# A fused attention and expert block: the experts' weights loaded behind the stores of all batches, one more batch normalised by VectorE, the later tiles' deviations taken earlier

## What is computed

```
h = layernorm(x) * (1 + ca) + sa
x = x + ga * attention(h, Wq, Wk, Wv)      # 16 heads of 8, one key/value head
h = layernorm(x) * (1 + cb) + sb
x = x + gb * experts(h)                    # 8 experts, the best two per token, 128 -> 512 -> 128
```

## Time and profile before

| | |
|---|---|
| three timed runs, median (lowest, highest) | 623.52 us (622.25, 624.11) |
| the profiled execution | 620.85 us |
| its span | 619.0 us |
| mean granted clock of TensorE | 0.971 |
| busy: TensorE, VectorE, ScalarE, GpSimd | 90%, 80%, 72%, 52% |

### The profile page before, as it was taken

How to read it: one execution, slowest core, us unless ns; L and a number is a source line. 1 busy time by engine, 2 the same in 40 slices (tenths; PEclk the granted TensorE clock), 3 DMA queues, 4 the chain that set the end, 5 groups by cost and what they waited for, 6 DMA issues and landing times.

```text
span 619.0 us, 18924 instructions
## 1 busy us (share of the span) xinstructions
PE 557.3 (90%) x6699; PEld 307.3 (50%) x6699; DVE 495.7 (80%) x1132; ACT 444.6 (72%) x776; POOL 323.1 (52%) x576
## 2 busy tenths in 40 slices
PE   3677999999999999999999999999889999899970
PEld 2222333443443343343343344343369998799970
DVE  5767999989789789879788888878767777656687
ACT  5575488888778788978887877878766555467771
POOL 2525101034455666667667666765417767755670
PEclk9797999999999999999999999999899999999995
DMA  7973400120120220230130030000123223232645
GB/s 197 334 230 115 131 8 12 41 66 13 41 64 19 67 72 17 54 84 18 36 103 18 22 109 21 23 27 26 45 57 99 76 83 95 84 100 68 200 137 174
DMA packets 49868, 49.32 MB, mean 80 GB/s; under 512 B 15616, under 2 KB 44336, under 8 KB 49056
## 3 DMA queue, kind: packets, MB, share of 16 engines
q1 hardware_dynamic: 42256, 36.89, 21.5%
q0 software_dynamic: 4320, 9.38, 4.6%
q10 hardware_dynamic: 3200, 1.84, 1.0%
HBM read 29.40 MB, written 17.10 MB: 75 GB/s over the span
## 4 chain that ended last, share of the span: by engine, by line
PE 68%; DVE 16%; ACT 6%; issue 3%; POOL 2%; DMA 2%; SPq 0%; POOLq 0%; DVEq 0%; ACTq 0%
PE ps L1095 15%; PE ps L1054 13%; PE ps L1085 12%; DVE neg_max L1400 10%; PE ps L1163 10%; PE ps L1174 9%; ACT P L1262 3%; ACT diag L1272 2%; PE ps L1122 1%; PE ps L1137 1%; PE ps L1154 1%; PE ps L1073 1%; POOL h_sorted L809 1%; DVE P L286 1%; PE ps L469 1%
## 5 line engine op out<-in xcount | busy, mean ns | idle before, releaser
L1400 DVE TENSOR_REDUCE neg_max<-ps 128x1 f32<-128x512 f32 x512 | 321.1, 683 | 54.5 <-PE ps L1054 53.5
L1262 ACT ACTIVATE P<-ps,zero 128x1024 f32<-128x1024 f32 x256 | 272.3, 1112 | 72.5 <-PE ps L1085 72.2
L1054 PE MATMUL ps<-K,Q 128*32 128x512 bf16 x2048 | 183.3, 383 | 4.9 <-DVE neg_max L1400 4.5
L1085 PE MATMUL ps<-Q,K 128*32 128x512 bf16 x2048 | 155.9, 381 | 5.5 <-ACT P L1262 5.1
L1095 PE MATMUL ps<-P,V 128*32 128x512 f32 x1024 | 134.1, 598 | 1.2 <-ACT P L1262 1.1
L1054 PEld LDWEIGHTS ps<-K,Q 128*32 128x32 bf16 x2048 | 54.5, 96 | 108.7 <-DVE neg_max L1400 59.8
L1612 POOL DMA_INDIRECT y_rows<-P,to_now x71 | 73.8, 1040 | 61.0 <-DVE P L1452 28.6
L1318 ACT ACTIVATE parts<-ps,parts 128x128 f32<-128x128 f32 x228 | 65.1, 371 | 40.3 <-PE ps L1163 40.3
L1085 PEld LDWEIGHTS ps<-Q,K 128*32 128x32 bf16 x2048 | 52.4, 97 | 75.6 <-issue 28.8
L809 POOL DMA_INDIRECT h_sorted<-diag,slot x64 | 64.8, 1013 | 28.6 <-POOL max_parts L79 13.4
L1163 PE MATMUL ps<-parts 128*128 128x128 f32 x456 | 61.0, 277 | 2.6 <-DVE parts L1433 1.3
(11 more groups left out here) (239 smaller groups left out, 583.3 us busy)
## 6 DMA issues: line engine op xcount, KB each, us to landing
Q<-q_parts SPq DMA_DIRECT2D x24, 384.0 KB
xs<-h_sorted SPq DMA_DIRECT2D x71, 72.0 KB
W<-w_t SPq DMA_DIRECT2D x2, 2048.0 KB, 10.7
q_parts<-parts SPq DMA_DIRECT2D x8, 384.0 KB, 3.9
Q<-y_rows SPq DMA_DIRECT2D x6, 512.0 KB, 4.5
diag<-att_u SPq DMA_DIRECT2D x128, 16.0 KB
Q<-max_parts SPq DMA_DIRECT2D x96, 4.0 KB, 1.8
out<-Q SPq DMA_DIRECT2D x6, 256.0 KB, 2.3
```

What stands on the lines that cost most here:

```text
L1054: ins = eng.matmul(ring_bank(*unit)[QUAD * q:QUAD * (q + 1), :], Q[buffer_of(g)][:, g % NG * G + j, at:at + QUAD], K[buffer_of(g)][:, 0, : ...
L1085: ins = eng.matmul(bank(2 * u + j)[QUAD * q:QUAD * (q + 1), :], K[p][:, 1, at:at + QUAD], Q[p][:, g % NG * G + 2 * u + j, :], start=True, ...
L1262: nc.scalar.activation(P[s % 2][:, 2 * u:2 * u + 2, :], bank(2 * u, 2).rearrange("p (j t) -> p j t", j=2), ACT.Exp, bias=zero[:], scale=SC ...
L1400: eng.tensor_reduce(neg_max[g % 2][:, j * T + s:j * T + s + 1], ring_bank("maximum", g, s, j), AX.X, ALU.max, negate=True).then_inc(ring_u ...
```

## The change

It has three parts. The four loads of the experts' weights move on SyncE from ahead of batch 0's store to behind the store of batch 7, and the two waits ahead of them go. `VECTOR_FIRST` becomes 4: VectorE normalises all four tiles of batch 3, and does so inside `take(0)`, between its two kinds of subtractions, no longer at the head of `take(1)`. The root of the later tiles' variances moves on ScalarE from behind `mid(1)` to behind `modulate(2)`, and its reciprocal on VectorE from ahead of `take(2)` to ahead of `take(1)`. The order of everything else stays.

```diff
-        VECTOR_FIRST = 3
+        VECTOR_FIRST = 4
...
-            eng.wait_ge(loaded, START + LOADED)
-            eng.wait_ge(x_arrived[-1], START + 16)
-            eng.dma_start(W1[:, :, 0:F], w1_t).then_inc(experts_loaded, 16)
-            eng.dma_start(W1[:, :, F:F + FC], b1_t).then_inc(experts_loaded, 16)
-            eng.dma_start(W2[:], w2_t).then_inc(experts_loaded, 16)
-            eng.dma_start(W1[:, :, F + FC:], b2.partition_broadcast(128)).then_inc(experts_loaded, 16)
             store(eng, 0)
             eng.wait_ge(cleared, START + 4)
             eng.wait_ge(stored[0], START + STORES)
             load_operands(eng, 0, 0, batch_loaded)
             for b in range(1, B):
                 store(eng, b)
+            eng.dma_start(W1[:, :, 0:F], w1_t).then_inc(experts_loaded, 16)
+            eng.dma_start(W1[:, :, F:F + FC], b1_t).then_inc(experts_loaded, 16)
+            eng.dma_start(W2[:], w2_t).then_inc(experts_loaded, 16)
+            eng.dma_start(W1[:, :, F + FC:], b2.partition_broadcast(128)).then_inc(experts_loaded, 16)
...
                 mid(b)
-                if b == 1:
+                if b + 2 < B:
+                    modulate(b + 2)
+                if b == 0:
                     eng.wait_ge(var1_done, START + 16)
                     deviations(LATER)
-                if b + 2 < B:
-                    modulate(b + 2)
                 if b + 1 < B:
                     hi(b + 1)
...
-                if b + 2 < B:
+                if b != 1 and b + 2 < B:
                     eng.wait_ge(var_done, known(b + 2))
                     eng.wait_ge(xT_done, START + b + 1)
                     normalize(eng, b + 2, first_xn, by_vector(b + 2))
...
                     eng.tensor_tensor(rest_of(b, n), projected(b, n), part(b, n, 0), ALU.subtract).then_inc(rest_done, 1)
+                if b == 0:
+                    eng.wait_ge(xT_done, START + 2)
+                    normalize(eng, 3, first_xn, by_vector(3))
...
             for b in range(B):
-                if b == 2:
+                if b == 1:
                     eng.wait_ge(std_done, START + 3)
                     eng.reciprocal(ln_rstd[:, LATER], ln_rstd[:, LATER]).then_inc(var_done, 1)
                 take(b)
```

## The result

| | before | changed |
|---|---|---|
| median of 5 timed runs (lowest, highest) | 623.52 us (622.25, 624.11) | 618.48 us (618.13, 620.76) |
| ratio to before, 95% interval | | 0.9924 (0.9908 to 0.9940) |
| the profiled execution, its span | 620.85, 619.0 | 618.48, 616.6 |
| mean granted clock of the profiled execution | 0.971 | 0.977 |

The changed kernel is faster by 5.0 us, 0.8%. The forecast was 619.6 us (616.8 to 622.6), a gain of 3.9.

A forecast was written before the change was run, and what follows sets the result against it. The opening stage, with TensorE's idle stretches and half clock, was taken to set the chain's end. Front 3.9 us, stores, reload, weights and later stages 0: 617.0 us against the profiled execution, 619.6 against the median, range 616.8 to 622.6.

The forecast's parts named there:

- What bounds the kernel: Whole span: TensorE carries 68% of the last-ending chain, DMA 2%; any gain comes from the opening stage and reaches the end.
- Batch 3 on VectorE: Opening stage: VectorE's tiles end near 22.15 us, so batch 3's transposes start at 22.2, 1.7 us earlier.
- GpSimd's tiles: Opening stage: two normalisations took 1.06 us each from 21.71; batch 4's two start at 23.4 and take 1.6 to 2.1.
- Deviations ahead: Opening stage: later tiles' reciprocal at 23.1 us without waiting; batch 4's transposes near 26.45 against 29.93, 3.5 us earlier.
- The clock: TensorE's turn for batch 4: full speed adds 1.65 us to 3.5, 5.1 in all; 3.9 taken, bounds 1.8 and 5.1.
- fourth rival: Behind 46 us: half clock lasts longer or falls in a busier place, 3.3 us eat nearly all the gain; chance 0.08.
- Weights behind the stores: SyncE's queue: removing four issues frees nothing that was ready, and the weights' new place costs 0; bounds -0.5 and +5 us.
- The reload and batch 1's store: SyncE: reload issued from 27.5 to 29 us, ahead of the first maximum; batch 7's copies about even, at worst 1 us.
- second rival: First maximum waits for batch 0's reload, or batch 7's copies for batch 1's store; gain 1.9 us, 621.6; chance 0.08.
- shift(0) behind the weights: SyncE's queue: its transfers queue behind the weights' rest, land near 63 us, wanted at 68.4; the 5 us gap hides it.
- Against the median: Whole kernel: the profiled execution lies 2.7 us under the median 623.52, so 617.0 becomes a forecast of 619.6 us.

## Why the prediction was right, and where not

- **What bounds the kernel.** Right. The two idle stretches, their causes and the half clock between them were where the gain was, and the attention handed the front's lead on to the experts' stage to a tenth of a microsecond.
- **Batch 3 on VectorE.** Right to 0.1 us: transposes forecast at 22.2, seen at 22.15; the idle stretch 1.06 us against 1.2.
- **GpSimd's tiles.** The reading of 1.06 us each was an average over unlike ones: one took 1.33 us, the other 0.79. After the change batch 4's two took 0.81 and 0.83 us, the lower end of the 1.6 to 2.1 allowed. The slow one (21.71 to 23.04) began beside VectorE's wide subtraction for the last parts (L418, 21.66 to 22.35), and so did every slow one in both front traces (1.0 to 1.33 us); beside VectorE's normalisations and first subtractions they took 0.79 to 0.86. So sharing shows here beside one kind of VectorE instruction and not beside the others.
- **Deviations ahead.** Right: reciprocal forecast at 23.1, seen at 22.92; batch 4's transposes 26.45, seen 26.30.
- **The clock.** The sum's mis-sized term. I took 3.9 us, near the floor; the profile gives 5.1 by the first maximum, the upper bound, because the 2.0 us idle stretch did not lower the clock. Three other profiles with the same front lost it there, so the edge was rightly seen and the side wrongly chosen. That the clock is worth this much is shown: with only the clock held and the old order, the gain by the ratios is as large. The fourth rival, a longer half clock behind the front, did not come: it lasted about 7 us both before (from 46.8) and after (from 42.2).
- **Weights behind the stores, priced 0.** Right for the move alone (0.2%), wrong for its part in the change, and hidden by a sum that came out near. The step read who waited for SyncE's row before and found nobody; it did not ask who would wait once the front is 4 to 5 us faster and the weights are still early. The run with the weights early shows it: by the ratios 3.7 of 4.7 us go. The move makes room for the gain rather than giving one, and so does issuing batch 1's store first.
- **The reload and batch 1's store** (second rival). The store landed in 2.4 us instead of the 4.7 assumed, so the reload started 1.1 to 2.6 us before the forecast's 27.5 to 29. "About even; at worst 1 us" for the copies of batch 7 was right: 0.6 us.
- **shift(0) behind the weights.** Forecast to land near 63 without being waited for. Its last transfer landed by 62.9 and nobody waited. The three took 3.1 to 3.5 us to land instead of 1.8, and so landed about when the last of the weights did (62.2), which is nearer to the queue's order than to mere sharing. Loads of this size can hold up a shift all the same, as the run with the weights further back shows, at a price of 14 us.
- **Against the median.** Right to go by it: the profiled execution of before was 2.7 us under it. 1.6 us of that fit the clock that stayed up in the experts' stage. The rest is not explained: timed executions of before with a higher mean clock (0.975) took 621.9 to 622.1 us, longer than this one with 0.971.

## What to carry to other kernels

Price a move by who would wait for it in the new schedule, not by who waits in the old: a load that nobody waits for becomes the bound as soon as the work beside it gets faster, and two edits worth 0.2% each can be worth 0.8% together. Where the granted clock falls in short idle stretches, look for the longest two and close both; a few unused matmuls in them are the cheap test of what the clock is worth. Before large loads are put into a queue, look at which small, urgent transfers are issued behind them, and put the loads where the next such transfer is furthest away.

## What the runs showed of the hardware

- Over an idle stretch of TensorE of 2.0 us between stretches of work the clock held in four profiles and fell in three with the same order of work (in 26 to 27 us 1.00 in the changed kernel, 0.56 and 0.51 in two of the runs). At a wait of 2.2 to 2.4 us in the experts' stage it held in the profile of before and fell in the eight others named. At one of 2.9 to 3.3 us in the front it fell in all four profiles that have one; at the one of 1.1 us in none.
- The clock need not fall inside the idle stretch: before, it fell in 22 to 23 us, ahead of the transposes at 23.92; with only the weights moved it fell in 24 to 25, when they had begun. What it then cost differed too, since it stayed low from 26.1 to 29.5 us in one run (batch 1's store first) and from 24.4 to 38.1 in another (weights moved).
- One of GpSimd's 128 by 128 normalisations took 0.79 to 0.86 us, and 1.0 to 1.33 when it ran beside VectorE's 128 by 512 subtraction for the last parts (before, from 21.71: 1.33; after, from 24.98: 1.19).
- Stores of 0.5 MB took 2.4 us from last issue to landing on empty queues, 5.8 behind the weights, and again 5.8 when issued behind a reload.
- SyncE's issue of a 2 MB load took 4.4 us behind another such load (in the changed kernel, from 47.13), and 9.3 behind a reload, a 0.6 MB fill and another such load (weights behind the second reload). The engine is held while it issues: what a queue costs can be time of the issuing engine, not only of the transfer.
